# Convolution and graph attention on one core: half stages with the same filling, and sums over slots as identity matmuls

## The reference

```
x = x + conv(layernorm(x))                 # conv ends in "+ its own input"
t = tokens(x); y = layernorm(t)
h = y @ W_gat                              # 4 heads x 4 experts = 16 numbers
e = leaky_relu(a_src[src] + a_dst[dst])    # 524,288 random edges and one loop a node
alpha = softmax of e over the edges with the same dst
agg = segment_sum(h[src] * alpha, dst)
scores = mean over heads of layernorm(agg + b_gat)
gate = softmax over the top 2 of 4 experts, the others 0
t = t + sum over experts of gate * (gelu(y @ W1 + b1) @ W2 + b2)
```

## Time and profile before

| | us |
|---|---|
| median of 3 runs | 2232.26 (2231.24 to 2236.48) |
| the profiled execution | 2230.75, its span 2229.1 |
| DVE busy | 1745.4 (78%) |
| POOL busy | 1184.2 (53%) |
| PE busy | 1092.5 (49%) |
| ACT busy | 769.8 (35%) |
| POOL's row gathers | 1,026, busy 1052.2 |
| ACT, one instruction (0 to 640 us) | norm or residual of a tile 0.49, copy of a chunk 0.59, its output 0.69, rewrite or relu of an image 1.11, node rows 0.25 |

### The profile page before, as it was taken

One profiled execution on the slowest core, in us unless ns is written; L12 is line 12 of the kernel. 1 busy time (PEld: TensorE's weight loads), 2 busy tenths in 40 slices (PEclk: granted clock), 3 DMA queues, 4 the chain that ended last, 5 costly groups with the idle time before them and its releaser, 6 DMA issues. The chain is left out here.

```text
span 2229.1 us, 16984 instructions
## 1 busy us (share of the span) xinstructions
PE 1092.5 (49%) x4914; PEld 492.6 (22%) x4914; DVE 1745.4 (78%) x3440; ACT 769.8 (35%) x1289; POOL 1184.2 (53%) x1167
## 2 busy tenths in 40 slices
PE   2886887787678899301600243342424241514230
PEld 1223343333453333100200021111101110202110
DVE  5999999998649999999383555868595859586868
ACT  4663854635245555200300133222313132313220
POOL 2000000000047777777776777777777777777760
PEclk9898888888669999755855576666767575757665
DMA  8301121021345222211220233252524342425252
GB/s 290 135 1 38 39 8 39 1 8 38 46 43 100 73 73 71 54 14 41 76 45 13 42 100 124 74 165 62 167 73 156 80 160 67 160 68 168 63 140 70
DMA packets 142649, 177.40 MB, mean 80 GB/s; under 512 B 64154, under 2 KB 115292, under 8 KB 132956
## 3 DMA queue, kind: packets, MB, share of 16 engines
q1 hardware_dynamic: 86988, 88.84, 13.9%
q0 software_dynamic: 40768, 42.44, 11.3%
q10 hardware_dynamic: 14800, 45.04, 5.2%
HBM read 99.82 MB, written 76.40 MB: 79 GB/s over the span
## 5 line engine op out<-in xcount | busy, mean ns | idle before, releaser
L534 POOL DMA_INDIRECT KC<-node_dram,KB x1026 | 1052.2, 1026 | 937.5 <-DMA node_dram<-node_out 625.1
L757 PE MATMUL hidden_out<-XT,W 128*128 128x512 f32 x512 | 290.6, 675 | 554.9 <-ACT ARENA_A L977 554.0
L762 PE MATMUL hidden_out<-ARENA_A,W 128*128 128x512 f32 x512 | 267.3, 648 | 24.9 <-ACT ARENA_A L977 24.9
L977 ACT ACTIVATE ARENA_A<-hidden_out,b1c 128x512 f32<-128x512 f32 x256 | 174.2, 687 | 245.3 <-PE hidden_out L757 244.7
L757 PEld LDWEIGHTS hidden_out<-XT,W 128*128 128x128 f32 x512 | 98.5, 213 | 703.7 <-ACT ARENA_A L977 583.2
L1695 DVE TENSOR_TENSOR KB<-KC,MB 128x320 f32<-128x320 f32 x66 | 29.2, 483 | 193.6 <-DMA KC<-payload,slot_idx 193.0
L1052 ACT ACTIVATE TA<-KB 128x320 f32<-128x320 f32 x64 | 26.0, 438 | 432.9 <-DVE KB L1705 432.8
L980 ACT ACTIVATE ARENA_A<-hidden_out,b2c 128x512 f32<-128x512 f32 x128 | 87.9, 687 | 188.3 <-PE hidden_out L762 188.3
L1867 DVE SCALAR_TENSOR_TENSOR XG<-XT,KB,XG 128x128 f32<-128x128 f32 x512 | 144.1, 346 | 3.7
L1711 DVE TENSOR_TENSOR KA<-KC,TA 128x1280 f32<-128x1280 f32 x66 | 95.2, 1483 | 56.9 <-ACT TA L1052 55.9
L762 PEld LDWEIGHTS hidden_out<-ARENA_A,W 128*128 128x128 f32 x512 | 98.4, 207 | 183.2 <-ACT ARENA_A L977 103.7
(11 more groups left out here) (407 smaller groups left out, 2140.3 us busy)
## 6 DMA issues: line engine op xcount, KB each, us to landing
ye_dram<-ARENA_D ACTq DMA_DIRECT2D x32, 1024.0 KB, 4.0
XT<-ye_dram SPq DMA_DIRECT2D x32, 1024.0 KB, 13.0
KC<-node_dram,KB POOLq DMA_INDIRECT x1026, 2.5
payload<-XT SPq DMA_DIRECT2D x1, 11520.0 KB
payload<-KC SPq DMA_DIRECT2D x115, 90.0 KB, 1.9
XG<-x_dram SPq DMA_DIRECT2D x32, 256.0 KB, 10.8
out_dram<-XG ACTq DMA_DIRECT2D x32, 256.0 KB, 2.9
KA<-in_L_ffn_edge_index_dram SPq DMA_DIRECT2D x1, 2048.0 KB, 9.0
```

What stands on the lines that cost most here:

```text
L534: pool.indirect_dma_start(row_buf[h][:, t, :], None, node_dram, bass.IndirectOffsetOnAxis(ap=KB[:, col:col + 1].bitcast(I32), axis=0)).the ...
L757: last = pe.matmul(PF[i % 2][:, :], W1[:, m // 2, (m % 2) * P:(m % 2) * P + P], XT[:, n * CHUNK:(n + 1) * CHUNK], start=True, stop=True)
L762: last = pe.matmul(PF[i % 2][:, :], W2[:, 2 * m + kk, :], HH[:, 2 * m + kk, :], start=kk == 0, stop=kk == 1)
L977: act.activation(HH[:, m, :], PF[i % 2][:, :], ACT.Gelu, bias=b1c[:, m:m + 1]).then_inc(S["hid_out"], 1)
```

## The change

Two parts. In the convolution phase the tables are new: every place of a group holds the same kinds of work, groups 1 to 3 the same amounts. A norm's second product comes behind the next half stage (`use_pending`, `pending_out`), the residual scaling is a step of its own (`keep`, KEEP_FILL), statistics may cover a part of a group (STATS1: group 0 in two parts; STATS2: group 3 in four), their variance comes from six operations on whole tensors instead of a bn_aggr a tile, and DVE's counts of sort steps are new. The eleven loads of the convolution's weights are issued on ACT's queue and have semaphores of their own; SP's queue holds x of group 0 in two halves, x of group 1, the edges, x of group 2 and then the twelve other weights. `small_weights` is a generator whose steps stand between bn_stats; the rest of it is now `later_weights` and `gat_weights`.

In the attention passes two halvings on DVE go. PE sums with `sum_slots`: five matmuls of the identity with 128x512 slices of the products, accumulated in the bank that held the running maximum, which moves to SBUF (`run_max_in`). DVE reduces what is left (four slots a node) in `summed_by_pe`, for the pass before and behind the scores of the next, or at the end of a super group. PE's experts are split in `hidden_layers` and `back_to_rows`, one of them ahead of each pass's sum.

The tables and parts:

```diff
-STEP3_FILL = ((0, 0, 0, 0, 0, 0, 0, 0), (2, 4, 2, 0, 0, 0, 0, 0), (2, 4, 2, 0, 0, 0, 0, 0), (2, 2, 2, 2, 0, 0, 0, 0))
-NORM_FILL = ((0, 2, 0, 2, 0, 2, 2, 0), (0, 0, 0, 3, 3, 3, 3, 4), (0, 0, 0, 3, 3, 3, 3, 4), (0, 0, 0, 0, 0, 2, 3, 3))
+STEP3_FILL = ((0,) * 8,) + ((2, 2, 2, 2, 0, 0, 0, 0),) * 3
+NORM_FILL = ((2, 1, 1, 1, 1, 1, 1, 0), (2,) * 8, (2,) * 8, (0, 0, 0, 0, 2, 2, 2, 2))
+KEEP_FILL = (2, 2, 2, 2, 0, 0, 0, 0)
-STEPS_AFTER = ((0, 2, 1, 1, 1, 2, 1, 0), (0, 4, 1, 1, 1, 4, 1, 0), (0, 4, 0, 4, 0, 4, 0, 0), (0, 1, 1, 1, 1, 1, 1, 0))
+STEPS_AFTER = ((0, 3, 0, 3, 0, 3, 0, 0), (0, 5, 0, 5, 0, 5, 0, 0), (0, 5, 0, 5, 0, 5, 0, 0), (0, 0, 1, 0, 1, 1, 1, 0))
+STATS1 = [(0, 0, 4), (0, 4, 8)] + [(g, 0, 8) for g in range(1, GROUPS)]
+STATS2 = [(g, 0, 8) for g in range(GROUPS - 1)] + [(GROUPS - 1, c, c + 2) for c in range(0, 8, 2)]
```

PE's norm of group 0, its places, and its sums in the passes:

```diff
+            for c in range(CHUNKS):
+                transposes(1)
+                if c == 1:
+                    pe.wait_ge(S["comp_dve"], 8)
+                if c:
+                    use_pending(1)
+            use_pending()
+            pe.wait_ge(S["conv_in"], 16 * N_CONV)
...
                     conv_half(g, place // 2, place % 2)
-                    if place == 0 and g >= 2:
-                        last_chunk()
+                    use_pending()
                     for c in islice(chunks, STEP3_FILL[g][place]):
                         step3(g - 1, c)
-                    norm_chunks(NORM_FILL[g][place])
+                    transposes(NORM_FILL[g][place])
...
+            def sum_slots(n):
+
+                pe.wait_ge(S["products_ready"], n + 1)
+                for k in range(0, SLOTS, SUMMED):
+                    last = pe.matmul(slot_sums, ident[:, :], each_product[:, :, k * HE:(k + SUMMED) * HE],
+                                     start=k == 0, stop=k + SUMMED == SLOTS)
+                last.then_inc(S["slots_summed"], 1)
...
+            chunks = iter(range(FIRST_CHUNKS, FFN_CHUNKS))
+            experts(next(chunks))
+            for n in range(NODE_GROUPS):
+                chunk = next(chunks, None) if n % 2 == 0 else chunk
+                if chunk is not None:
+                    (hidden_layers, back_to_rows)[n % 2](chunk)
+                sum_slots(n)
```

ACT's places:

```diff
             for g in range(GROUPS):
+                for place in range(8):
+                    i = place // 2
+                    if place % 2 and i < 3:
                         rewrite(g, i)
+                    if place == 4 and g:
                         root2(g - 1)
+                        first_norms(2, g - 1)
+                    place_work(g, place)
+                    if place % 2:
+                        relu(g, i)
+                    for c in range(KEEP_FILL[place]):
+                        keep(g, sum(KEEP_FILL[:place]) + c)
+                    if place == 4 and g < 2:
+                        root1(g + 3)
+                if g < 2:
+                    first_norms(1, g + 2)
```

DVE's `variances`, its order as it is now, and its part of the passes:

```diff
-                for t in range(TILES):
-                    last = dve.bn_aggr(mean_var[:, t, :], bn[:, t, :])
-                link(last)
-                ts(std[:, :], mean_var[:, :, 1], eps, None, ALU.add).then_inc(S[ready], 1)
+                tt(twice, bn[:, tiles, 1], bn[:, tiles, 4], ALU.add)
+                tt(std[:, tiles], bn[:, tiles, 2], bn[:, tiles, 5], ALU.add)
+                link(tt(spread, bn[:, tiles, 1], bn[:, tiles, 4], ALU.subtract))
+                ts(std[:, tiles], std[:, tiles], 1.0 / C, eps, ALU.mult, ALU.add)
+                link(tt(spread, spread, spread, ALU.mult))
+                stt(std[:, tiles], spread, 0.25, std[:, tiles], ALU.mult, ALU.add).then_inc(S[ready], 1)
...
+            small = small_weights()
+            token_stats(0, small)
             scales1(0)
+            token_stats(1, small)
+            scales1(1)
+            token_stats(2)
+            later_weights()
             keys = make_keys()
             next(keys)
+            scales1(2)
             next(keys)
+            gat_weights()
+            token_stats(3)
+            sort_steps(8)
+            scales1(3)
             sort_steps(4)
             residual(0)
             scales2(0)
+            sort_steps(5)
+            token_stats(4)
+            sort_steps(4)
+            scales1(4)
+            sort_steps(13)
             residual(1)
             scales2(1)
+            sort_steps(26)
             residual(2)
             scales2(2)
+            sort_steps(33)
             residual(3)
+            scales2(len(STATS2) - 1)
             sort_steps(ROW)
...
                     scores(slot_rows[h], cols, link).then_inc(S["e_ready"], 1)
+                    if n > groups[0]:
+                        summed_by_pe(n - 1)
                     dve.wait_ge(S["e_exp"], n + 1)
-                    sums(slot_rows[h], cols, link).then_inc(slots_used[h], 1)
+                    products(slot_rows[h], cols, link, "products_ready")
+                    denominators(cols, link).then_inc(slots_used[h], 1)
                     dve.wait_ge(slots_used[h], n // 2 + 1)
+                summed_by_pe(groups[-1])
```

More of the change, by code:

```diff
@@ L118, with part_of @@
 ROUND_MAGIC = 12582912.0
+STATS1 = [(0, 0, 4), (0, 4, 8)] + [(g, 0, 8) for g in range(1, GROUPS)]
+STATS2 = [(g, 0, 8) for g in range(GROUPS - 1)] + [(GROUPS - 1, c, c + 2) for c in range(0, 8, 2)]
+def part_of(parts, g, c):
+    return next(k for k, (h, first, end) in enumerate(parts) if h == g and first <= c < end)
 def trips_before(n):
@@ L750, in _, with hidden_layers @@
-            last_chunk()
-            def experts(n):
+            transposes(2)
+            for c in range(6, CHUNKS):
+                step3(GROUPS - 1, c)
+            for _ in range(3):
+                use_pending(2)
+                transposes(2)
+            use_pending()
+            def hidden_layers(n):
                 done = n * len(LAYERS)
@@ L844, in norm, with keep @@
                 last.then_inc(S["y_ready"], 1)
[L845 to L850, removed]
+            def keep(g, c):
+                for t in range(TPC):
+                    tt = TPC * c + t
+                    last = act.activation(x_tile(g, tt), x_tile(g, tt), ACT.Identity,
+                                          scale=scale1x[g % 2][:, tt:tt + 1], bias=shift1[g % 2][:, tt:tt + 1])
+                last.then_inc(S["xres_ready"], 1)
             def copy_chunk(n):
@@ L887, in chunk_out, with root, root1, root2 @@
                                    ACT.Copy).then_inc(S["node_out_done"], 1)
[L889 to L895, removed]
+            def root(std, parts, k, var, ready):
+                g, first, end = parts[k]
+                tiles = slice(first * TPC, end * TPC)
+                act.wait_ge(S[var], k + 1)
+                act.activation(std[:, tiles], std[:, tiles], ACT.Sqrt).then_inc(S[ready], 1)
+            def root1(k):
+                root(std1, STATS1, k, "var1_ready", "std1_ready")
+            def root2(k):
+                root(std2, STATS2, k, "var2_ready", "std2_ready")
             def rewrite(g, i):
@@ L930, in last_chunk, with pending_out, norms, place_work @@
-            def last_chunk():
-                chunk_out(next(out))
+                    pending.append(n)
+            def pending_out(count=NORMS):
+                for _ in range(min(count, len(pending))):
+                    chunk_out(pending.pop(0))
+            normed = [0]
+            def norms(end):
+                while normed[0] < min(end, NORMS):
+                    norm(normed[0])
+                    normed[0] += 1
+            def place_work(g, place):
+                pending_out()
+                first = sum(sum(row) for row in NORM_FILL[:g]) + CHUNKS + sum(NORM_FILL[g][:place])
+                for n in range(first, first + NORM_FILL[g][place]):
+                    copies(1)
+                    kind, h, c = NORM_ORDER[n]
+                    if c < CHUNKS - 2:
+                        norms(n + 3)
@@ L973, in hidden @@
+            pending_out()
+            root2(GROUPS - 1)
+            for k in range(GROUPS - 1, len(STATS2)):
+                norms(norm_at[(2, GROUPS - 1, 0)] + 2 * (k - GROUPS + 2))
+                copies(2)
+                if k + 1 < len(STATS2):
+                    root2(k + 1)
+                pending_out()
             def hidden(n):
@@ L1086, in _, with token_stats @@
             dve.wait_ge(S["consts"], 10)
-            def token_stats(g):
-                dve.wait_ge(x_in[g], 16 * len(x_parts[g]))
-                for t in range(TILES):
+            def token_stats(k, between=iter(())):
+                g, first, end = STATS1[k]
+                if g:
+                    dve.wait_ge(x_in[g], 16 * len(x_parts[g]))
+                else:
+                    dve.wait_ge(x_first_in[k], 16)
+                for t in range(first * TPC, end * TPC):
                     last = dve.bn_stats(bn[:, t, :], x_tile(g, t))
+                    if t % 2:
+                        next(between, None)
@@ L1093, in token_stats @@
```

(1 more changed line is left out.)

232 lines of the change are left out of this document (118 added, 114 removed).

## The result

The changed kernel takes 2207.27 us (median of 4 runs, 2206.27 to 2215.17) where the kernel before, run beside it, takes 2232.53 (2231.24 to 2236.48): a ratio of 0.9893, 95% interval 0.988 to 0.9905. It is 25 us faster; 56 were forecast, and the range ended at 2205.

A forecast was written before the change was run, and what follows sets the result against it. POOL's issue of indirect DMAs was taken as the bound: its start, its 1,150 DMAs, and what follows. 2230.75 - 34 - 24 + 2 = 2175, with the median 2176; range 2158 to 2205.

The forecast's parts named there:

- the sum of DVE's waits: Convolution phase: DVE's waits up to the sort's end total 20 us (8 to 45), so the sort ends at 596.
- Rival (a): Convolution keeps DVE waiting through ACT's in-order waits: 35 to 60 us of waits, 2191 to 2216, some 2198; chance 0.20.
- DVE's work: Convolution phase and sort: DVE's work without waits falls from 573 to 566.5 us.
- The twelve variance blocks: Convolution statistics: six operations each on at most 128x32, 1.1 us a block, so 13 us added to DVE.
- PE's first convolution: Start of the convolution phase: it starts at 43 instead of 66.79, wrong above 52.
- The way from the sort to POOL: Between sort and gathers: POOL starts 5 us after the sort, at 601, instead of 18.6 after it.
- The row gathers: Attention passes: without DVE's adds POOL's gathers are no longer stretched, -24 us (0 to -26), mean near 0.965 us.
- The end: After pass 30's slot gather: DVE waits for PE's sums in the last two super groups, +2 us (0 to +7).
- Rival (b): Attention passes: not the adds but something beside them stretches the gathers; time 2200, chance 0.12.
- (c): Convolution phase: DVE waits less than counted, as at residual(0); time 2162 and below, chance 0.08.
- (d): Convolution phase: ACT becomes the bound and the kernel gets slower, 2282 at 4 us a half stage; chance 0.05.
- the first term: When POOL's first gather starts, after sort and node rows: net -34 us (-9 to -46).

The follow-up runs named there:

- e3: The changed kernel with sort steps moved to where DVE waits for ACT's roots, the same steps in all: 2177.45 us (0.9763).
- e7: e4 with the three DVE adds put back behind the reduction, their results read by nobody: 2245.20 us (1.0058).
- e8: e4 with the products of exp and rows taken twice, one input in PSUM: 2213.22 us (0.9915).
- e4: The kernel before, with one DVE reduction over all 40 slots replacing three adds and a reduction over five; no TensorE sums: 2204.48 us (0.9881).
- e2: The kernel before (its convolution phase kept) with the sums on TensorE: 2210.70 us (0.991).

## Why the prediction was wrong

**The step that failed** is the sum of DVE's waits, "Roots and small weights 3; group 3's four part statistics, each a trip over ACT, 4. Sum 20 us (8 to 45)", from which the sort's end at 596 follows. The sum was 45.8, above even its upper bound, and the sort ended at 625.5. Of the 25.8 too many the roots make 21 (27.9 in the four long waits, against 7 for roots, small weights and parts together), residual(1) 5.9 where none was forecast, residual(0) 2 (11 instead of 9), and the load of group 3 gives 3 back (1.1 instead of 4).

The roots were priced as trips over ACT, about 1 us each. But DVE waits until ACT has worked off what stands ahead of the root in its queue. ACT around the first of these waits, then DVE (its variance ends at 199.72, the next row is the reciprocal):

```profile
199.38 4.50 ACT L976 ACTIVATE XT<-hidden_out,cb 32x1024 f32<-32x1024 f32 x4
203.91 3.20 ACT L908 ACTIVATE ARENA_D<-ARENA_D,shift,scale1x 128x128 f32<-128x128 f32 x8
207.01 0.21 ACT L954 ACTIVATE std<-std 128x32 f32<-128x32 f32 x1
```

```profile
199.53 0.19 DVE L1192 SCALAR_TENSOR_TENSOR std<-mean_var,std 128x32 f32<-128x32 f32 x1
207.26 0.35 DVE L1214 RECIPROCAL scale<-std 128x32 f32<-128x32 f32 x1 [7.53 <-ACT std L954]
```

The written order has root2 at place 4, behind the relu of four images (4.50 us) and two chunks of `keep` (3.20). DVE asks for it at 199.7, and between `residual(0)` and `scales2(0)` the change has nothing, where the kernel before had 12 sort steps. The prediction weighs whether DVE's residuals are behind PE, and not what DVE does in the instruction after them. The wait at 340 is the same (7.54). Those of 6.47 and 6.32 us at 557.5 and 565.2 are a circle: ACT's queue holds a part's root behind the norm of the part before and the node rows of the part before that. PE's products for the first of these rows need the PSUM banks that DVE frees with the residuals of chunks 6 and 7, and right behind chunk 7 DVE waits for the root, twice. The first time, on DVE, PE, ACT and DVE again:

```profile
549.48 0.69 DVE L1224 TENSOR_TENSOR KC<-KC,MB 128x512 f32<-128x512 f32 x1
...
550.31 1.87 PE L695 MATMUL MB<-node_w,XT 128*128 128x24 f32 x8 [4.74 <-DVE KC L1224]
...
552.22 0.25 ACT L945 ACTIVATE node_out<-MB 128x96 f32<-128x96 f32 x1 [6.36 <-PE MB L695]
...
557.24 0.20 ACT L954 ACTIVATE std<-std 128x8 f32<-128x8 f32 x1
557.54 0.20 DVE L1214 RECIPROCAL scale<-std 128x8 f32<-128x8 f32 x1 [6.47 <-ACT std L954]
```

The second root stands behind the next part's node rows, norm and copies on ACT, and comes 7.8 us later (565.01).

Rival (a), "ACT's in-order waits", had the size (waits of 35 to 60, up to 2216) at a chance of 0.20, but at other places, a rewrite behind a keep and root1(4) behind x; its upper half was left out of the range.

e3 is the test: with the four waits covered the sort ends at 596.2, POOL starts at 601.2 and the time is 2177.45, against 596, 601 and 2176 of the forecast. That they meet so closely is in part luck: e3's waits are 16.6 us where 20 were forecast, DVE's work is 4 us more than forecast, and e3 is not the kernel that was forecast.

**The other steps.**

- DVE's work: 573.7 us with its small gaps before and 570.7 after, 3.0 less where 6.4 were forecast. Its busy time fell by 6.0, and the gaps of under 0.35 us grew by 3.1. The twelve variance blocks take 11.1 us, each from its first start to its last end, against 13.
- PE's first convolution starts at 44.64 (43 forecast). DVE's start at 9.0 is right.
- The way from the sort to POOL: 625.5 to 630.5, the forecast 5 us, released by DVE's mask. POOL's first window gather comes 17.1 us behind its first row gather instead of 14.2, so 2.9 us are lost there, where 3 were forecast.
- The row gathers: 25.8 us in the passes, 24 forecast, at a mean of 0.962 us. The mechanism was named rightly: e7 and e8, with as much added to DVE at the same place, show it. (The prediction's 61 gathers are those that start in an add; 91 overlap one.) The Trainium skill (SBUF — State Buffer, Who interferes with whom) says that a DVE instruction with at most one SBUF input, outside the 2-port perf modes, does not contend with GpSimd; e4 and e8 agree, with means of 0.959 and 0.962 us. Its inference that descriptor generation is not stalled by tensor_tensor would have left these gathers alone, and 0.95 us became 2.07. Whether such a gather is held where it reads its offsets or at descriptor generation, no run here separates.
- The end: 75.6 us from pass 30's slot gather to the end before, 82.2 after, 6.6 more where 2 were forecast (0 to 7). I took "five identity matmuls" at 1.04 us after idling and so 5.2 us, but in the trace each of them is two instructions, and the ten take 7.6 and 7.2 us. PE's sum of a pass behind other work, then in passes 30 and 31:

```profile
2125.55 4.56 PE L806 MATMUL MB<-KA,ident 128*128 128x512 f32 x10 [1.57 <-DVEq L1824]
2141.34 7.64 PE L806 MATMUL MB<-KA,ident 128*128 128x512 f32 x10 [11.23 <-DVEq L1824]
2183.10 7.24 PE L806 MATMUL MB<-KA,ident 128*128 128x512 f32 x10 [34.13 <-DVEq L1824]
```

DVE waits for them twice at the end, once for each of the last two super groups:

```profile
2149.08 0.69 DVE L1840 TENSOR_REDUCE KB<-MB 128x64 f32<-128x512 f32 x1 [6.16 <-PE MB L806]
...
2190.45 0.69 DVE L1840 TENSOR_REDUCE KB<-MB 128x64 f32<-128x512 f32 x1 [5.74 <-PE MB L806]
```

The granted clock is 1.00, the level of 2.4 GHz, during the first of these sums (2125.5 to 2130.1). In passes 30 and 31 it is 1.2 GHz for most of the sum, 0.59 and 0.63 in the mean (2141.3 to 2149.0, 2183.0 to 2190.4), after 11 and 34 us in which PE did nothing. The 4.56 us divided by these give 7.7 and 7.2, so the clock accounts for the difference.

Rival (b) fell with e7; (c) is out with 45.8 us of waits, and (d), since the sort's end moved by 6 us and not by 33. Most of the miss is the first term's 29 us; without the tail's 5 the time would have been just inside the range, at 2203, and still 27 us from the forecast. With the roots covered, and the sums still on TensorE, e3 takes 2177; in its trace the tail is 78.7 us, 2.5 of the 3.5 less because the slot rows of pass 30 come sooner (6.35 us behind their issue instead of 8.89).

## What to carry to other kernels

A wait on another engine costs what stands ahead of it in that engine's queue, not the length of the instruction waited for: for each wait, list what the other engine does at that moment, and put work that is anyway to be done between the request and the use. When an engine that only issues is the bound, look at whether its instructions have all the same length; where they are stretched, what runs beside them can be worth as much as what stands in front of them. And before work goes to another engine, ask whether the gain comes from where it goes or only from what it leaves: here one reduction on the same engine, 0.86 us a pass slower than the adds with theirs (4.43 against 3.57), gave at least what TensorE gave (2204 in e4, 2211 in e2).

## What the runs showed of the hardware

An indirect DMA on POOL, 0.94 us long, is held when it starts while DVE runs an f32 add with both inputs in SBUF (2.07 us beside adds of 1.49 and 0.82 us; of before's row gathers in the passes 61 such carry 24.0 us, and 30 that were already running carry nothing), and not by a reduction with one input in SBUF (0.95 us beside 4.43 us of it) nor by a product with its second input in PSUM (0.95 us beside 2.88). In every run the gathers before the passes, which run beside the sort of list 1 with its minima and maxima of two SBUF inputs, keep a mean of 1.06 us; no experiment took that up. An f32 matmul of 128x512 against the identity shows as two instructions, of 0.46 us each behind other work at a granted clock of 1.00 (4.56 us for ten) and 0.76 us each after 11 us of idling, at a mean granted clock of 0.59 (7.64 us for ten).
